# Experts' second layer in 32-row tiles, and ScalarE square roots in the tail's norms

## The reference, cut to what matters

```python
x = x + attention(layernorm(x), ctx)                 # 16 heads
x = x + experts(layernorm(x))
x = x + mlstm(layernorm(x), ctx, gates)              # 8 heads, then an RMS norm per head
x = x + bitffn(layernorm(x))                         # 8-bit activations, ternary weights, hidden 2048, exact gelu

# experts: 32 experts e with 4 sets s; perm picks for each (e, s) one token of each group of 32
permuted = einsum('bntd,bntes->bnesd', grouped, perm)
inner = relu(einsum('bnesd,esdf->bnesf', permuted, W1) + b1)      # f = 32 inner values
result_permuted = einsum('bnesf,esdf->bnesd', inner, W2) + b2     # the second layer
result = einsum('bnesd,bntes->bntd', result_permuted, perm)

# layernorm: (x - m) / sqrt(v + 1e-5)
# mlstm's end, per token and head: h = hf * rsqrt(mean(hf**2) + 1e-6)
```

## Time and profile before

| | |
|---|---|
| time, median of 3 runs | 2611.24 us (2610.79 to 2611.46) |
| profiled execution: time | 2620.14 us |
| profiled execution: span from first to last instruction | 2618.4 us |
| mean granted clock of PE | 0.902 of 2.4 GHz |
| PE busy | 2216.2 us (85%) |
| DVE busy | 1524.9 us (58%) |
| ACT busy | 1347.6 us (51%) |
| POOL busy | 616.1 us (24%) |

### The profile page before, as it was taken

One profiled execution on the slowest core, in us unless ns is written; L12 is line 12 of the kernel. 1 busy time (PEld: TensorE's weight loads), 2 busy tenths in 40 slices (PEclk: granted clock), 3 DMA queues, 4 the chain that ended last, 5 costly groups with the idle time before them and its releaser, 6 DMA issues. The chain is left out here.

```text
span 2618.4 us, 43758 instructions
## 1 busy us (share of the span) xinstructions
PE 2216.2 (85%) x14571; PEld 1398.9 (53%) x14571; DVE 1524.9 (58%) x2958; ACT 1347.6 (51%) x2952; POOL 616.1 (24%) x1020
## 2 busy tenths in 40 slices
PE   7999999999999999678788449696979797979755
PEld 3666666666666666375484127353535353535432
DVE  2767676767676767423323225766666666666664
ACT  3666565656565655223324237564646454555543
POOL 1332323131323132031120012313131313131310
PEclk9999999999999999889999767797979797979777
DMA  6334343434343333166756764222122222222100
GB/s 189 95 102 137 82 137 84 138 81 139 78 142 81 109 79 103 49 176 175 239 158 201 257 237 170 97 69 81 68 81 68 81 68 81 68 81 68 37 13 17
DMA packets 193553, 289.05 MB, mean 110 GB/s; under 512 B 29440, under 2 KB 93984, under 8 KB 188128
## 3 DMA queue, kind: packets, MB, share of 16 engines
q1 hardware_dynamic: 134384, 200.32, 24.2%
q10 hardware_dynamic: 42608, 52.97, 6.4%
q0 software_dynamic: 16384, 33.59, 5.0%
HBM read 156.62 MB, written 63.05 MB: 84 GB/s over the span
## 5 line engine op out<-in xcount | busy, mean ns | idle before, releaser
L499 DVE TENSOR_REDUCE a_negmax<-a_score 128x1 f32<-128x512 f32 x512 | 346.5, 685 | 117.2 <-PE a_score L614 109.0
L434 ACT ACTIVATE a_prob<-a_score,a_negmax 128x512 f32<-128x512 f32 x512 | 354.2, 694 | 94.4 <-DVE a_negmax L499 93.5
L316 POOL DMA_DIRECT2D a_q_stack<-a_q_parts x512 | 250.8, 498 | 513.1 <-DVE a_q_parts L493 253.8
L614 PE MATMUL a_score<-a_k_stack,a_q_stack 128*128 128x512 f32 x512 | 354.6, 693 | 9.5 <-ACT a_prob L434 7.6
L622 PEld LDWEIGHTS a_turn<-a_ident,a_prob 128*128 128x128 f32 x2048 | 254.2, 141 | 134.6 <-issue 93.2
L622 PE MATMUL a_turn<-a_ident,a_prob 128*128 128x128 f32 x2048 | 309.3, 274 | 3.4 <-ACT a_perm L410 2.0
L324 DVE COPY a_probT<-a_turn 128x512 f32<-128x512 f32 x256 | 176.4, 689 | 215.8 <-PE a_turn L622 215.6
L324 ACT COPY a_probT<-a_turn 128x512 f32<-128x512 f32 x256 | 150.2, 587 | 285.3 <-PE a_turn L622 283.7
L1253 POOL TENSOR_SCALAR c_diag<-c_negm,c_aL 128x128 f32<-128x128 f32 x256 | 165.5, 664 | 362.2 <-DVEq L1474 127.5
L1711 PE MATMUL c_work<-c_xT,c_cT 64*128 64x512 f32 (+3 forms) x512 | 185.2, 510 | 39.7 <-DVE c_decay L1480 39.7
L1711 PEld LDWEIGHTS c_work<-c_xT,c_cT 64*128 64x128 f32 x512 | 105.2, 215 | 138.7 <-issue 74.4
(11 more groups left out here) (196 smaller groups left out, 3732.8 us busy)
## 6 DMA issues: line engine op xcount, KB each, us to landing
a_k_stack<-a_k_parts SPq DMA_DIRECT2D x512, 64.0 KB, 2.7
a_q_stack<-a_q_parts POOLq DMA_DIRECT2D x512, 64.0 KB, 2.3
scratch_res<-b_res SPq DMA_DIRECT2D x32, 1024.0 KB, 4.6
c_res<-scratch_res SPq DMA_DIRECT2D x32, 1024.0 KB, 9.6
b_xn<-scratch_xn SPq DMA_DIRECT2D x68, 256.0 KB, 2.7
c_hid<-in_L_ffn_W ACTq DMA_DIRECT2D x16, 1024.0 KB, 5.1
c_negm<-scratch_m SPq DMA_DIRECT2D x64, 256.0 KB, 3.4
a_xs<-in_x ACTq DMA_DIRECT2D x8, 1024.0 KB, 5.3
```

The source lines that it names most:

```text
L316: eng.dma_start(stack[kind][i * DH0:(i + 1) * DH0, M % 2, g, :].bitcast(F32), parts[kind][g * DH0:(g + 1) * DH0, part, :].bitcast(F32)).th ...
L434: nc.scalar.activation(prob[:, U % 4, :], score.bank(U)[:, :], ACT.Exp, bias=negmax[:, u:u + 1], accum_out=sums[:, head_of(U), tile_of(U): ...
L499: nc.vector.tensor_reduce(negmax[:, U % UNITS:U % UNITS + 1], score.bank(U)[:, :], AX.X, ALU.max, negate=True).then_inc(max_ready, 1)
L614: nc.tensor.matmul(score.bank(U)[:, :], stack["Q"][:, M % 2, g, t * P:(t + 1) * P], stack["K"][:, M % 2, g, :], start=True, stop=True).the ...
```

## The change

The second layer takes a set's 32 partitions of `inner` against the same 32 rows of `w2T`, so that the four products of an expert lie in four row tiles of PE. `inner` loses its axis of sets, its zeros and the fill on POOL; relu is one instruction for an expert over all 128 partitions. PE now waits for all four banks before the first of the four products. In the tail a new class `RootNorm` takes the place of `Norm` for both norms: DVE signals the variance, ACT writes sqrt(variance + eps), DVE takes the reciprocal. The RMS norm over the heads is done alike. Attention keeps `Norm`.

```diff
+class RootNorm:
+    def moments(self, dve, chain, last):
+
+        chain.step(last, apart=True)
+        for t in range(T):
+            last = self.nc.vector.bn_aggr(self.mv[:, t, :], self.stats[:, t, :])
+        chain.step(last, apart=True)
+        dve.sem_inc(self.var_ready, 1)
+
+    def scale(self, dve, chain, b):
+
+        dve.wait_ge(self.std_ready, b + 1)
+        chain.step(self.nc.vector.reciprocal(self.rstd[:, :], self.std[:, :]))
+
+    def on_scalar(self, act, b):
+        act.wait_ge(self.var_ready, b + 1)
+        self.nc.scalar.activation(self.std[:, :], self.mv[:, :, 1], ACT.Sqrt,
+                                  bias=self.eps[:, 0:1]).then_inc(self.std_ready, 1)
...
-        inner = sb("inner", [P, 2, NE, SETS, G])
+        inner = sb("inner", [P, 2, NE, G])
...
-                nc.gpsimd.memset(inner[:, :, :, :, :], 0.0).then_inc(zeroed, 1)
-
...
                                 for s in range(SETS):
                                     work.wait_free(pe, h * WORK + GATHERED, 4 * e + s)
-                                    nc.tensor.matmul(work.bank(s)[:, :], inner[:, (j - 1) % 2, e % NE, s, :], w2T[:, e % 2, :],
+                                for s in range(SETS):
+                                    r = slice(s * F, (s + 1) * F)
+                                    nc.tensor.matmul(work.bank(s)[:, :], inner[r, (j - 1) % 2, e % NE, :], w2T[r, e % 2, :],
                                                      start=True, stop=True).then_inc(work.full[s], 1)
...
                             for e in range(NE):
-                                for s in range(SETS):
-                                    r = slice(s * F, (s + 1) * F)
-                                    last = nc.scalar.activation(inner[r, j % 2, e, s, :], aux.bank(j)[r, e * G:(e + 1) * G], ACT.Relu,
-                                                                bias=b1c[r, bass.ds(h * XH + (j * NE + e), 1)])
+                                last = nc.scalar.activation(inner[:, j % 2, e, :], aux.bank(j)[:, e * G:(e + 1) * G], ACT.Relu,
+                                                            bias=b1c[:, bass.ds(h * XH + (j * NE + e), 1)])
...
-        norm0, norm1 = Norm(ctx, sems, nc, "c_norm0"), Norm(ctx, sems, nc, "c_norm1")
+        norm0, norm1 = RootNorm(ctx, sems, nc, "c_norm0"), RootNorm(ctx, sems, nc, "c_norm1")
...
                 for n in range(3):
                     sum_weight(n)
+                norm0.on_scalar(act, 0)
                 front_copies(None, 0, "XT")
...
+                        if next_too and h == H1:
+                            norm0.on_scalar(act, m + 1)
+                    if m is not None:
+                        act.wait_ge(meansq_ready, m + 1)
+                        nc.scalar.activation(f2[:, :, :], f2[:, :, :], ACT.Sqrt, bias=eps6[:, :]).then_inc(rms_ready, 1)
                     if next_too:
                         front_copies(m, J_FRONT, "XT")
                         front_copies(m, J_FRONT, "CT")
+                    if m is not None:
+                        norm1.on_scalar(act, m)
+                    if next_too:
                         front_logs(m + 1, m, J_FRONT)
...
-                    step(nc.vector.tensor_tensor(f2[:, :, :], f2[:, :, :], f1[:, :, :], ALU.mult))
-                    inverse_root(nc, step, f3[:, :, :], f2[:, :, :], 1e-6, f4[:, :, :], f5[:, :, :])
+                    nc.vector.tensor_tensor(f2[:, :, :], f2[:, :, :], f1[:, :, :], ALU.mult).then_inc(meansq_ready, 1)
+                    dve.wait_ge(rms_ready, m + 1)
+                    step(nc.vector.reciprocal(f3[:, :, :], f2[:, :, :]))
```

More of the change, by code:

```diff
@@ L184, in on_vector, with __init__, tile_stats, tile_result @@
         return last
+class RootNorm:
+    def __init__(self, ctx, sems, nc, name):
+        self.nc = nc
+        sb = lambda n, shape: ctx.enter_context(nc.sbuf_tensor(f"{name}_{n}", shape, F32))
+        self.stats, self.mv, self.rstd = sb("stats", [P, T, 6]), sb("mv", [P, T, 2]), sb("rstd", [P, T])
+        self.std = sb("std", [P, T])
+        self.eps = sb("eps", [P, 1])
+        self.var_ready = sems.make(f"{name}_var_ready")
+        self.std_ready = sems.make(f"{name}_std_ready")
+    def tile_stats(self, src, t):
+        return self.nc.vector.bn_stats(self.stats[:, t, :], src[:, t, :])
+    def moments(self, dve, chain, last):
[7 more added lines that the diff above has]
+        chain.step(self.nc.vector.reciprocal(self.rstd[:, :], self.std[:, :]))
+    def tile_result(self, src, dst, t):
+        return self.nc.vector.tensor_scalar(dst[:, t, :], src[:, t, :], self.mv[:, t, 0:1], self.rstd[:, t:t + 1],
+                                            ALU.subtract, ALU.mult)
+    def on_vector(self, dve, chain, b, src, dst):
+        for t in range(T):
+            last = self.tile_stats(src, t)
+        self.moments(dve, chain, last)
+        self.scale(dve, chain, b)
+        for t in range(T):
+            last = self.tile_result(src, dst, t)
+        return last
+    def on_scalar(self, act, b):
+        act.wait_ge(self.var_ready, b + 1)
+        self.nc.scalar.activation(self.std[:, :], self.mv[:, :, 1], ACT.Sqrt,
+                                  bias=self.eps[:, 0:1]).then_inc(self.std_ready, 1)
 def attention_phase(nc, sems, A, scratch):
@@ L776, in experts_phase @@
         b1_in, b1_ready = sem("b1_in"), sem("b1_ready")
-        zeroed = sem("zeroed")
         xn_in = [sem(f"xn_in{t}") for t in range(T)]
@@ L943, in _ @@
                 act.wait_ge(b1_ready, 2)
-                act.wait_ge(zeroed, 1)
                 w2_d = A["L0_ffn_W2"].rearrange("(h e) s (p c) f -> h e p s (c f)", h=HALVES, c=C)
@@ L1054, in tail_phase @@
         b1, b2 = sb("b1", [P, HID]), sb("b2", [P, D])
-        one = sb("one", [P, 1])
+        one, eps6 = sb("one", [P, 1]), sb("eps6", [P, 1])
         rnd = sb("rnd", [P, 1])
@@ L1072, in tail_phase @@
         hraw = sb("hraw", [P, T, PAIRS, 2 * DH1 + 2])
-        f1, f2, f3, f4, f5 = (sb(f"f{k}", [P, T, H1]) for k in range(5))
+        f1, f2, f3 = (sb(f"f{k}", [P, T, H1]) for k in range(3))
         square, sumsq = sb("square", [P, T, DH1]), sb("sumsq", [P, T, H1])
@@ L1099, in tail_phase @@
         shifted, masked, decay_ready = sem("shifted"), sem("masked"), sem("decay_ready")
-        squares_ready = sem("squares_ready")
+        squares_ready, meansq_ready, rms_ready = sem("squares_ready"), sem("meansq_ready"), sem("rms_ready")
         xq_ready, x3_read, bias_added = sem("xq_ready"), sem("x3_read"), sem("bias_added")
@@ L1233, in _ @@
                 for tile, value in ((v[:, :, :, 0:1], 1.0), (v[:, :, :, 2 * DH1 + 1:2 * DH1 + 2], 1.0), (one[:, :], 1.0),
-                                    (rnd[:, :], ROUND)):
+                                    (eps6[:, :], 1e-6),
+                                    (norm0.eps[:, :], LN_EPS), (norm1.eps[:, :], LN_EPS), (rnd[:, :], ROUND)):
                     nc.gpsimd.memset(tile, value).then_inc(filled, 1)
@@ L1268, in _ @@
             def _(act):
-                act.wait_ge(filled, 4)
+                act.wait_ge(filled, 7)
                 act.wait_ge(const, 2)
@@ L1516, in normalize_x2 @@
                     norm0.moments(dve, chain, last)
-                    norm0.scale(chain)
+                    norm0.scale(dve, chain, m)
                     for t in range(T):
@@ L1540, in front_rows @@
                     nc.vector.tensor_scalar(row(3), row(3), -1.0, None, ALU.mult).then_inc(m_ready, 1)
-                FIRST_STEPS, STEPS = 4 + ROOT_STEPS, 28 + 3 * ROOT_STEPS
+                FIRST_STEPS, STEPS = 5, 30
                 chain = Chain(dve, dve_chain, 0, FIRST_STEPS)
@@ L1625, in turn @@
                     step(last)
-                    step(norm1.on_vector(dve, chain, x3, x2))
+                    step(norm1.on_vector(dve, chain, m, x3, x2))
                     dve.sem_inc(x3_read, 1)
@@ L1649, in _ @@
                 pe.wait_ge(gkv_ready, 1)
-                pe.wait_ge(filled, 4)
+                pe.wait_ge(filled, 7)
                 def transposes(banks, b, j, src_of, bf=False):
```

## The result

| | before | after |
|---|---|---|
| time, median of 4 runs each | 2611.35 us (2610.79 to 2613.85) | 2542.74 us (2539.34 to 2545.40) |
| ratio, 95% interval | 1 | 0.9735 (0.9718 to 0.9752) |
| profiled execution: time, span | 2620.14, 2618.4 us | 2539.34, 2537.4 us |
| clock of PE | 0.902 | 0.890 |
| start of the tail's block | 1485.6 us | 1463.5 us |

The kernel is faster by 2.65%, 69 us, where 73 were forecast. But the two profiled executions put the gain elsewhere than the forecast did: 22 us ahead of the tail in place of 35, and 59 in the tail in place of 38.

A forecast was written before the change was run, and what follows sets the result against it. Bounds: PE's waits for relu and weights in the experts' second stage, DVE's path to `xq` in the tail. Experts 33.6, fill 1.4 and tail 37.7 sum to 72.7 us off 2611.2: 2538 us, range 2518 to 2570.

The forecast's parts named there:

- Relu (a): Experts' second stage: a quarter as many relus, each lasting as long, 1.5 us a group in place of some 5.9.
- The set of four (b): Experts' second stage: an expert's four products run side by side in row tiles, 1.1 us in place of 3.60.
- The steps within a group (b): Second stage, expert to expert: 3.7 us in place of 4.0, ten undisturbed steps a half, 3.0 us a half.
- The circle: Second-layer weights' issue, landing at POOL, turning on PE, products, copies: two steps, 7.97 us, forecast to fall to 6.9.
- Steps that stay at 4.0 since the transfers don't come sooner: Sign named as proving the forecast wrong: expert steps in the second stage not falling to 3.7 us.
- Between groups (c): Second stage, group ends: gains of 1.7, 2.5, 4.1 and 5.5 us for the first, second, third and last group.
- The fill (d): Before the experts: dropping POOL's 3.51 us fill of `inner` ahead of the masks gives 0 to 3.5 us, taken as 1.4.
- The clock rival: PE's clock falls in the experts' second stage, so they gain only 6.8 us in all: 2565 us, chance 0.18.
- Roots (tail): Tail: three roots of 2.38 to 2.69 us become 0.7 to 0.9, gaining 5.4 us a turn, 32.4 over six.
- The root that waits for a weight copy in turn 0: Tail, turn 0: table load and Sqrt follow ACT's weight copy, a loss of 1.9 us; turn nets 1.8 gained.
- The cover of the logarithm: Tail, turn's end: the gates' Exp reloads its tables, 1.28 us, yet the logarithm ends 2.3 us before `xq`.
- Open loads: Rival: table loads begin only when the variance is there, 1.28 us at each norm0, 9.0 in all: 2547.5 us, chance 0.08.

The follow-up runs named there:

- the narrow relu kernel: The changed kernel with each expert's relu again taken in four pieces of 32 partitions, 16 a group in place of 4; 2564.17 us, ratio to before 0.9791.
- the kernel with PE kept busy: The changed kernel with two products that nothing reads behind each expert's four in the second stage; 2542.75 us, ratio to before 0.9703.

## Why the forecast was right, and where it was not

The total came out (2542.7 against 2538) since two terms were off in opposite directions: some 14 to 22 us from the experts in place of 35, some 49 to 59 from the tail in place of 38. That they nearly cancelled was luck.

**Relu (a): right in size, too large in effect.** 0.38 us each, 1.5 a group in place of 5.9. On the path the 4.4 us were worth only some 2 to 3 a group (the narrow relu kernel); that the next weights are on their way meanwhile is the likely reason.

**The set of four (b): right.** 1.14 us against 1.1 forecast, at full clock. 3.60 / 1.14 is 3.2. The Trainium skill (TensorE: Matmul & The Clock Gate, Measured speedup) has 3.07 for this form; the trace is near it.

**The steps within a group (b): this is the step that failed.** "I take 3.7 between 3.4 and 4.0." The circle was the right one, but the forecast took the time from issue to POOL over from the earlier trace rows. It became 6.21 us in place of 3.82, and the circle of two steps 10.3 us (1256.16 to 1266.48) in place of 7.97: 2.39 from the set to the issue in place of 2.98, 6.21 to POOL, and 1.72 from there to the products in place of 1.17, since the turning ran at the low clock. The late half of the load is the one beside which the store of the results now starts. The 3.99 us taken for a step came from one quiet pair: the ten steps had a mean of 4.5 in before. These ten steps were to give 3.0 us a half and took 5.0 more: from the timelines, the steps within groups without the first and that of the late weights sum to 45.2 us before and 50.2 after. "Steps that stay at 4.0 since the transfers don't come sooner" was named as what could go wrong; they went above.

**Between groups (c): nearly right.** From the last set of a group to the next group's first it is 6.69, 6.65 and 5.16 us in place of 9.55, 9.55 and 9.54: a gain of 10.1 us where 11.3 were forecast. The first and the third group have the same rows in before (9.55 us, with 1.74 of waiting for relu), yet the forecast gave them 1.7 and 4.1; both gained 2.9. The forecast's sum for the third was 5.5; with a set of 2.09 and a first layer of 4.15 it became 6.7. The second group's late weights cost 6.38 in place of 9.88: 3.5 against 2.5. The first step of all, which the forecast left alone, lost 3.3 (8.25 in place of 4.99). From first set to last a half thus gained 5.4 in the first half, and from the same rows of the second half about 9; from a half's first relu to the next half's first relu, or to the tail's start, it is 10.5 and 13.3. Forecast were 16.8 each.

**The fill (d): wrong, it gave nothing back.** It was gone, and PE's first gather product came at 1118.35 in place of 1120.68. But SP's issue of the first weights, which stands ahead of the second batch of tokens, then took longer. SP's queue before and after:

```profile
1118.10 6.05 SPq L812 DMA_DIRECT2D b_w<-in_L_ffn_W  x4
1124.78 3.89 SPq L803 DMA_DIRECT2D b_xn<-scratch_xn  x1
```
```profile
1118.51 9.80 SPq L861 DMA_DIRECT2D b_w<-in_L_ffn_W  x4
1128.82 2.24 SPq L852 DMA_DIRECT2D b_xn<-scratch_xn  x1
```

PE's second batch started at 1138.98 in place of 1136.34, and the first relu at 1198.45 in place of 1196.76. From the issue of the first weights to PE's second batch it is 18.1 to 18.2 us in the three kernels with before's experts, and 18.7 to 20.5 in the eleven others. That the earlier gather is the cause is my reading; no kernel tests it alone.

**The clock rival** was right in what it said of the clock (0.67 in the stage, the sets at 2.09) and wrong as a cause: the kernel with PE kept busy takes it away and is not told apart from after. Its sum charges the third group 1.1 us and leaves out the first, which has the same rows.

**Roots (tail): right in size.** 0.73 us from variance to result at the first norm, 0.7 forecast. From `xn` to `xq`, where two of the roots stand, a turn lost 3.9 us, forecast 1.8 + 1.9 = 3.7. Turn 0 and the time before it gained 3.0 us up to the first `xq` (177.7 to 174.7 us from the tail's start), forecast 2.2, and the part behind the last loop turn 3.0, forecast 3.1. The root that waits for a weight copy in turn 0 is there: DVE waits 3.99 us for it.

**The cover of the logarithm: right, and thinner.** At two of the five loop boundaries DVE waits some 1.5 us for it, where it is otherwise idle for 0.7:

```profile
2118.54 0.74 DVE L1587 TENSOR_SCALAR c_gate_rows<-c_work,c_gb 8x512 f32<-8x512 f32 x1 [1.59 <-ACT c_gate_rows L1381]
```

**What the forecast for the tail lacked.** A loop turn gained 8.8 us, not 5.4. By the table: 3.9 from `xn` to `xq`, 3.7 from `c_aL` to `xn`, 1.2 from `xq` to `c_aL`. In the second, the first norm's root was to give 1.7; another 1.5 is PE's busy time, which in before's turns is 79.6 or up to 83.2 us at 0.88 to 0.92 (81.8 in the mean) and in after's 80.3 or 80.4, at 0.90 in each. The rest is in PE's waits and is not taken apart. The two windows of before that answer to after's above:

```profile
1930.62:2020.61 89.99, 82.89 (x439) 50.14 (x438) 49.51 (x97) 57.58 (x128) 25.72 (x40) 0.88 0.28 96
2060.02:2146.68 86.66, 79.56 (x439) 49.02 (x438) 49.40 (x98) 57.58 (x128) 25.72 (x40) 0.92 0.29 100
```

That turns flip between these two is also the likeliest reason for the spread of before's times. The third, 1.2, is DVE at the end of the loop's body. Before, then after:

```profile
2051.05 0.74 DVE L1531 TENSOR_SCALAR c_gate_rows<-c_work,c_gb 8x512 f32<-8x512 f32 x1 [3.19 <-issue]
```
```profile
1998.18 0.74 DVE L1587 TENSOR_SCALAR c_gate_rows<-c_work,c_gb 8x512 f32<-8x512 f32 x1 [0.70 <-DVE c_xq L1694]
```

DVE waited 3.2 to 3.5 us there in each loop turn with all three roots on it, and, but for its waits for the logarithm, 0.70 to 0.76 with two, with one, and with none. The wait is not in proportion to the body's length; it comes between two roots and three. Of its 2.5 us a turn only 1.2 show in the stretch from `xq` to `c_aL`.

**Open loads:** not so in the loop. In the loop turn shown above the load lies in ACT's wait for the variance, with 2.33 us to spare.

## What to carry to other kernels

When an engine's work in a circle shrinks, ask what else the circle then starts at the same moment: half of a load that took 2.8 us took 5.2 in the denser order, where the store had moved up to it by 0.3 us, and the steps got longer though the engines had less to do. A median over both halves of the load did not show this; the single transfers did. Asking for the weights one step sooner gave 32 us here, more than the engines' shorter work. And read off the trace what a held transfer really waits for: the wait added here held the store behind another load than the one meant.

Time several small cuts on one path together and one by one. Three roots of 1.7 to 1.9 us each gave 8.8 us a turn together, and 0.7 or 0.9 when only one of them was put back, since PE's clock and an engine's loop end moved with them.

## What the hardware showed that I had not expected

**A clock that decides a turn.** The 440 instructions of a stretch keep PE busy for 79.6 us at 0.92 and 82.9 at 0.88 (with 16 added products beside them 77.4 at 0.98), and the turn follows. 24 products that nothing reads, 6.5 us of PE's time in the timeline, made a turn of 119.3 us 3.5 us shorter in the new tail; in the old one they changed nothing that can be told in the time.

**A pause at the end of a long loop body.** The 3.19 us for which DVE waits for "issue" in before lie behind the branch that closes its loop's body: the branch ends at 2048.14, and DVE's next instruction of any kind comes 2.7 us later. In all 15 such turns of the three kernels with three roots by DVE this gap is 2.7 to 3.1 us, in after and with two roots 0.2 to 0.3. A queue for instructions carries one packet in the pause (at 2049.08) and one just behind it (2051.47); at the same place in after there is none. Over the loop turns (1670 to 2430 us) the rows of that queue are, before and after:

```profile
q14 instruction: 31, 0.25, 0.1%
```
```profile
q14 instruction: 6, 0.05, 0.0%
```

The kernel with two roots on DVE has 6 as well, those with three all have 31, five a turn. So the pause and the packets come together, and both with the third root. The Trainium skill (Advanced Engine Details and Errata, ISA Cache) says that an engine holds only two cache lines of 256 instructions each; a body that no longer fits would have to fetch at each turn. The traces agree in that the packets come at every turn with the third root and not without it. They do not bear out the figure: the records of DVE in a turn, its branches, register and semaphore instructions among them, are 345 in before, 327 with two roots and 282 in after, all below 512, though a trace need not hold every instruction. So the fetch stays a reading.

**A wide relu costs what a narrow one does**: 383 ns on 128 partitions, 360 on 32, both of 128 columns.
